# One attention layer on one core: the first stage in another order, weighted sums in one run, transposes three slots behind their scores

## The reference

```
# block 0: an adapter with one of 16 experts per sequence, then a layer norm
h   = gelu(x @ down_W.T + down_b)                 # 256 -> 64
h   = h @ expert_W[e].T + expert_b[e] + domain_emb[e]
x   = layernorm(h @ up_W.T + up_b + x) * gamma + beta
# block 1: attention with a bias, 16 heads of 16, then a feed-forward net
emb = silu(sin_cos(timestep)) @ W_ada + b_ada     # one row per sequence
x   = layernorm(x) * (1 + scale) + shift          # scale, shift = halves of emb
s   = q @ k.T / 4 + attention_bias                # 512 x 512 per head
p   = softmax(where(mask, -inf, s))
x   = x + (p @ v) @ Wo + bo
h   = layernorm(x) * g2 + beta2
out = x + gelu2(h @ W1 + b1) @ W2 + b2            # 256 -> 1024 -> 256
```

## Time and profile before

| | |
|---|---|
| median of three runs | 978.33 us (977.5 to 978.37) |
| profiled execution, its own time | 975.33 us |
| its span, first to last instruction | 973.4 us |
| PE busy | 904.8 us (93%) |
| DVE, ACT, POOL busy | 720.6, 702.2, 704.1 us (74, 72, 72%) |
| granted PE clock, mean | 0.972 of full speed |
| moved by DMA | 207.39 MB |

### The profile page before, as it was taken

How to read it: one execution, slowest core, us unless ns; L and a number is a source line. 1 busy time by engine, 2 the same in 40 slices (tenths; PEclk the granted TensorE clock), 3 DMA queues, 4 the chain that set the end, 5 groups by cost and what they waited for, 6 DMA issues and landing times.

```text
span 973.4 us, 20669 instructions
## 1 busy us (share of the span) xinstructions
PE 904.8 (93%) x6472; PEld 652.3 (67%) x6472; DVE 720.6 (74%) x1905; ACT 702.2 (72%) x1661; POOL 704.1 (72%) x407
## 2 busy tenths in 40 slices
PE   4648979999999999999999999999999999999986
PEld 1435545777677776777777776777777777677765
DVE  5738787878778787878778787878778787675642
ACT  2237758978788787878788787878788787877641
POOL 2448966888779886888769877878688886885700
PEclk8777989999999999999999999999999999999998
DMA  5499858876897669876797768876897668865300
GB/s 170 130 286 319 268 151 237 252 227 200 243 287 214 209 207 247 254 223 206 223 290 216 225 205 253 246 218 207 236 278 204 204 203 248 247 200 154 115 12 11
DMA packets 147948, 207.39 MB, mean 213 GB/s; under 512 B 14385, under 2 KB 62322, under 8 KB 147842
## 3 DMA queue, kind: packets, MB, share of 16 engines
q1 hardware_dynamic: 147842, 206.09, 71.7%
HBM read 185.05 MB, written 20.99 MB: 212 GB/s over the span
## 4 chain that ended last, share of the span: by engine, by line
PE 77%; DVE 2%; issue 2%; POOL 1%; ACT 1%; DVEq 0%; POOLq 0%; ACTq 0%
PE tp L834 19%; PE pv L791 12%; PE la L754 11%; PE sc L827 11%; PE lc L739 10%; PE lb L591 4%; PE lb L771 3%; PE lb L607 2%; DVE xm L1091 1%; PE lc L573 1%; POOL bias_s L494 1%; PE la L581 1%; PE la L565 1%; PE lb L565 1%; PE pv L802 1%
## 5 line engine op out<-in xcount | busy, mean ns | idle before, releaser
L494 POOL TENSOR_TENSOR bias_s<-mask_f,bias_s 128x1024 f32<-128x1024 f32 x256 | 602.3, 2371 | 159.6 <-DMA bias_s<-in_bias 159.0
L1360 DVE CUSTOM_DVE_ANT_0 bias_s<-sc,bias_s 128x512 f32<-128x512 f32 x512 | 349.1, 684 | 178.7 <-PE sc L827 166.1
L974 ACT ACTIVATE bias_s<-bias_s,mx 128x512 f32<-128x512 f32 x512 | 371.4, 726 | 115.9 <-DVE mx L1360 113.9
L834 PE MATMUL tp<-ident,bias_s 128*128 128x128 f32 x2048 | 311.6, 275 | 6.1 <-ACT pT L980 3.1
L834 PEld LDWEIGHTS tp<-ident,bias_s 128*128 128x128 f32 x2048 | 253.0, 142 | 87.3 <-issue 17.0
L980 ACT COPY pT<-tp 128x512 f32<-128x512 f32 x336 | 195.7, 583 | 91.2 <-PE tp L834 90.9
L827 PE MATMUL sc<-stk,stq 128*128 128x512 bf16 x512 | 197.3, 386 | 24.9 <-DVE mx L1360 20.4
L791 PE MATMUL pv<-pT,v_all 128*32 128x256 f32 x2048 | 138.4, 388 | 0.2 <-issue 0.2
L754 PE MATMUL la<-w_s,act_s 128*128 128x256 f32 x512 | 128.2, 380 | 0.2 <-DVE act_s L1317 0.2
L1367 DVE COPY pT<-tp 128x512 f32<-128x512 f32 x176 | 120.5, 684 | 4.3 <-PE tp L834 4.2
L739 PE MATMUL lc<-hT,w_s 128*128 128x256 f32 x464 | 120.8, 384 | 2.3 <-ACT hT L929 1.9
(11 more groups left out here) (172 smaller groups left out, 809.9 us busy)
## 6 DMA issues: line engine op xcount, KB each, us to landing
bias_s<-in_bias SPq DMA_DIRECT2D x256, 512.0 KB, 4.4
stq<-q_parts SPq DMA_DIRECT2D x128, 96.0 KB, 3.8
stk<-k_parts SPq DMA_DIRECT2D x128, 96.0 KB, 4.1
k_parts<-kb SPq DMA_DIRECT2D x32, 192.0 KB, 2.3
q_parts<-qb SPq DMA_DIRECT2D x32, 192.0 KB, 2.5
xT<-in_x_t SPq DMA_DIRECT2D x8, 512.0 KB, 6.2
k_parts<-kb SPq DMA_DIRECT2D x32, 128.0 KB, 2.3
stq<-q_parts SPq DMA_DIRECT2D x64, 64.0 KB, 4.0
```

Of the source, the lines that this page charges most:

```text
L494: pool.tensor_tensor(tile, mask_f[:, :, :], tile, ALU.subtract).then_inc(s["masked"], 1)
L834: last = pe.transpose(tp[n % 2][:, kt * P:(kt + 1) * P], bias_s[:, n // 2 % NB, n % 2, kt * P:(kt + 1) * P], ident[:, :])
L974: act.activation(tile, tile, ACT.Exp, bias=mx[:, t:t + 1], scale=-1.0, accum_out=sums[:, j, head_of(hh):head_of(hh) + 1]).then_inc(s["prob ...
L1360: dve.tensor_tensor_reduce(out=tile, in0=sc[t % 2][:, :], in1=tile, scale=1.0, scalar=BIG, op0=ALU.add, op1=ALU.min, accum_out=mx[:, t:t + ...
```

## The change

The change has five parts.

1. **Weighted sums in one run.** `weigh(g)` issues all 32 matmul records of a group at once, at 13.6, 21.6, 29.6 and 5.6. What follows it (spread, divide) stands a slot or less earlier.
2. **LAG = 3.** Each tile is transposed three slots behind its score. DVE_MOVES is shifted by one so that DVE moves stand in the same slots. In the last iteration DVE also moves tile 30.
3. **W1 preparation.** `shift_parts` and the eight `b1_diag` products leave iteration 1 and stand at the end of DVE's first stage.
4. **First stage in another order.** The seven other experts are prepared and folded before the norms end and not after the queries. Their copies go to ACT. The embedding product stands behind them. Weights for keys, queries and values are loaded from ACT's queue. SP loads the keys of a chunk as soon as its own stores have landed; ACT stores the first queries and loads them back. ACT computes one exponential of known values behind the second gelu, which brings the exponential's table in.
5. **Middle steps.** The row statistics `st2` no longer wait for ACT's copy `a_x2`, and the copy is issued behind `mv2`.

```
-LAG = 4
+LAG = 3
-DVE_MOVES = (8, 10, 11, 13, 15, 17, 20, 23, 24, 25, 27)
+DVE_MOVES = (9, 11, 12, 14, 16, 18, 21, 24, 25, 26, 28)
+LAST_DVE_MOVES = DVE_MOVES + (30,)
...
-             pv=((14.0, 15.0), (22.0, 23.0), (30.0, 31.0), (6.0, 7.0)), spread=(23.3, 7.3))
+             pv=(13.6, 21.6, 29.6, 5.6), spread=(22.3, 6.3))
...
-MID = dict(wo=(21.0, 21.6), x2=22.6, copy=23.0, st2=23.6, mv2=24.3, hn=27.0, ht=28.6)
+MID = dict(wo=(21.0, 21.6), x2=22.6, st2=23.6, mv2=24.3, copy=25.0, hn=27.0, ht=28.6)
...
-W1_AT = dict(parts=4.6, diag=(5.6, 12.0, 13.3, 14.6), sums=(18.0, 19.0), scale=(20.3, 21.3), lift=(22.0, 23.0))
+W1_AT = dict(sums=(18.0, 19.0), scale=(20.3, 21.3), lift=(22.0, 23.0))
...
+            def load_half_keys(b, g, e):
                 wait(sp, s["sc_ready"], TI * (2 * b - 1) + TG * (g + 1))
-                sp.wait_ge(s["k_out"], 64 * (2 * b + 2))
+                sp.wait_ge(k_out[g % 2], 32 * (2 * b + e + 1))
...
             store_keys(0)
-            store_queries(0)
+            load_half_keys(0, 0, 0)
             store_keys(1)
-            load_queries(0, 0)
-            load_keys(0, 0)
+            load_half_keys(0, 0, 1)
...
-                    for kt in range(2 * half, 2 * half + 2):
+                    for kt in range(KT):
...
             adapter_gelu(1)
+            act.activation(sm[:, 13, :], sm[:, 12, :], ACT.Exp, scale=-1.0)
             copy_rows(0)
+            copy_rows(1)
             keys(0, 0)
...
+            dve.wait_ge(s["experts_in"], 16 * (B - 1))
+            effective(1, B, "eff")
             center(0)
             center(1)
+            modulation()
             normalize(0)
...
             values(0)
+            shift_parts()
+            for ft in range(FT):
+                ins = dve.tensor_scalar(b1_diag[:, ft, :], ident[:, :], vec[:, VEC["b1"] + ft:VEC["b1"] + ft + 1],
+                                        None, ALU.mult)
+            ins.then_inc(s["w1_parts"], 1)
```

More of the change, by code:

```diff
@@ L77, in mid_at @@
     if m == NCH - 2:
[L78 removed]
+        at = dict(wo=(10.0, 10.3), x2=11.6, st2=12.3, mv2=13.3, copy=14.0, hn=16.0, ht=17.3)
     if m == NCH - 1:
[L80 removed]
+        at = dict(wo=(9.6, 10.0), x2=10.3, st2=10.6, mv2=11.0, copy=11.3, hn=12.0, ht=12.3)
     return absolute(at, m + 1)
@@ L121, in on_act @@
 def on_act(n):
-    return n % TI not in DVE_MOVES
+    return n % TI not in (LAST_DVE_MOVES if n // TI == NCH - 1 else DVE_MOVES)
 def moved(n, by_act):
-    return sum(on_act(k) == by_act for k in range(n % TI)) + n // TI * (21 if by_act else 11)
+    return sum(on_act(k) == by_act for k in range(n))
 def head_of(hh):
@@ L312, in build @@
         stk_in = [sem(f"stk_in{g}") for g in range(NG)]
+        k_out = [sem(f"k_out{m}") for m in range(2)]
         block = ctx.enter_context(nc.Block())
@@ L634, in _ @@
             turn_experts(0, 1, "turned0")
-            embedding()
             pe.wait_ge(s["up_in"], 32)
@@ L641, in _ @@
             adapter_up(1)
+            pe.wait_ge(s["eff"], 1)
+            turn_experts(1, B, "turned")
+            embedding()
+            pe.wait_ge(s["spread"], 1)
+            fold_expert(1, tp[1], 1)
+            for b in range(2, 4):
+                fold_expert(b, sc[1], b % 2)
+            for b in range(4, 6):
+                fold_expert(b, lb, b % 2)
+            for b in range(6, 8):
+                last = fold_expert(b, lc, b % 2)
+            last.then_inc(s["fold_sum"], 1)
+            pe.wait_ge(s["folded"], 2)
+            adapter_down(1, 0)
+            adapter_down(1, 1)
             turn_rows(0)
+            turn_rows(1)
             pe.wait_ge(s["k_w_in"], 16)
@@ L646, in _ @@
             keys(0, 1)
-            turn_rows(1)
+            pe.wait_ge(s["a_xt1"], 2)
+            keys(1, 0)
+            keys(1, 1)
             pe.wait_ge(s["scaled"], 1)
@@ L659, in _ @@
             values(0, 1)
-            adapter_down(1, 0)
-            adapter_down(1, 1)
-            pe.wait_ge(s["spread"], 1)
-            fold_expert(1, la, 0)
-            for b in range(2, 4):
-                fold_expert(b, sc[0], b % 2)
-            for b in range(4, 6):
-                fold_expert(b, pv, b % 2)
-            pe.wait_ge(s["d_q"], 1)
-            for b in range(6, 8):
-                last = fold_expert(b, tp[0], b % 2)
-            last.then_inc(s["fold_sum"], 1)
-            pe.wait_ge(s["folded"], 2)
-            pe.wait_ge(s["d_k"], 2)
+            pe.wait_ge(s["d_k"], 2)
+            pe.wait_ge(s["d_q"], 1)
             pe.wait_ge(s["d_v"], 1)
@@ L793, in weigh @@
                                              stop=(g % 2 == 1 and kt == KT - 1), tile_position=(0, 32 * h))
-                    if half == 1:
-                        last.then_inc(s["pv_done"], 1)
+                    last.then_inc(s["pv_done"], 1)
                 def spread_inverses(r):
@@ L814, in steps @@
                     for g in range(NG):
-                        if (prev if g == NG - 1 else attn) and t in AT["pv"][g]:
-                            weigh(g, AT["pv"][g].index(t))
+                        if (prev if g == NG - 1 else attn) and t == AT["pv"][g]:
+                            weigh(g)
                     for r in range(2):
@@ L889, in keys, with load @@
                     act.copy(kb[c % 2][:, 1, :], k_bank(c)[:, :]).then_inc(s["a_k1"], 1)
+            def load(sem_name, pairs):
+                for dst, src in pairs:
+                    act.dma_start(dst, src).then_inc(s[sem_name], 16)
+            act.wait_ge(s["vec_in"], 64)
+            load("norm_in", [(gamma_r[:, :], gamma.to_broadcast([P, D])), (beta_r[:, :], beta.to_broadcast([P, D]))])
+            load("k_w_in", [(wk_s[:, :, :], wk.rearrange("(c p) n -> p c n", p=P))])
+            load("q_w_in", [(wq_s[:, :, :], wq.rearrange("(c p) n -> p c n", p=P))])
+            load("v_w_in", [(wv_s[:, :, :], wv.rearrange("(c p) n -> p c n", p=P)),
+                            (bo_r[:, :], bo.to_broadcast([P, D])), (bv_r[:, :], bv.to_broadcast([P, D]))])
+            adapter_gelu(0)
             act.wait_ge(s["idx_ready"], 2)
@@ L899, in _ @@
             act.activation(wqf, wqf, ACT.Identity, scale=-0.25).then_inc(s["scaled"], 1)
+            act.wait_ge(s["fold_sum"], 2)
+            act.copy(fold[:, 1, :], tp[1][0:A + 1, D:2 * D])
+            act.copy(fold[:, 2:4, :].rearrange("p b d -> p (b d)"), sc[1][0:A + 1, :])
+            act.copy(fold[:, 4:6, :].rearrange("p b d -> p (b d)"), lb[0:A + 1, :])
+            act.copy(fold[:, 6:8, :].rearrange("p b d -> p (b d)"), lc[0:A + 1, :]).then_inc(s["folded"], 1)
+            adapter_gelu(1)
+            act.activation(sm[:, 13, :], sm[:, 12, :], ACT.Exp, scale=-1.0)
             copy_rows(0)
+            copy_rows(1)
             keys(0, 0)
-            copy_rows(1)
             keys(0, 1)
+            keys(1, 0)
             queries(0, 0)
+            keys(1, 1)
             queries(0, 1)
-            keys(1, 0)
-            keys(1, 1)
-            adapter_gelu(1)
+            act.wait_ge(s["d_q"], 1)
+            for m in range(2):
+                act.dma_start(q_d[0, m].rearrange("n p t -> p n t"), qb[:, :, m * CH:(m + 1) * CH]
+                              ).then_inc(s["q_out"], 16)
+            act.wait_ge(s["q_out"], 32)
+            for row, parts, _ in RUNS:
+                act.dma_start(stq[row:row + parts * HD, 0:GH, :], q_rows[0, 0, 0:parts * HD, 0:GH, :]
+                              ).then_inc(stq_in[0], 16)
             def body(i, attn, prev, nxt, pre, qv, down):
```

114 lines of the change are left out of this document (42 added, 72 removed).

## The result

The changed kernel takes 961.66 us (median of four runs, 960.01 to 964.4) where the kernel before takes 977.91 us on the same chip: a ratio of 0.9837, 95% interval 0.9811 to 0.9864. It is faster by 16.2 us; 24.3 us were forecast. The profiled execution took 960.01 us, its span is 958.2 us. PE is now busy 890.0 us where it was 904.8 us.

A forecast was written before the change was run, and what follows sets the result against it. PE's own instructions bound late iterations, transfers iteration 0, and a chain over all engines the first stage. Terms 13.4 + 0.5 + 8.5 + 0 + 0 + 1.9 = 24.3 us took the median from 978.33 to 954.0 us, range 946.5 to 961.5.

The forecast's parts named there:

- W1's preparation: Iteration 1: moving DVE's W1 work to the first stage, away from POOL, saves 8.5 us, bounds 6.5 and 12.
- Weighted sums in one run: Iterations 2 to 15: one entry and exit fewer saves 0.24 us a group, 13.4 us; iterations 0 and 1 add 0.5.
- LAG = 3 at nothing: Loop: transposing a slot sooner costs nothing, covered by slack of 0.7 us in the worst tile; bounds 2.2 us lost, or 0.
- The end: Kernel's end: st2 no longer waits 0.65 us and one slot less is owed, 1.2 us; together 1.9 us saved.
- Iteration 0 at nothing: Iteration 0: transfers bind it and their bytes and order stay, so 0 us; bounds -4 to +2.
- The first stage at nothing, bounds of 3 us: Up to the first score: late modulation and gains sum to about +0.6 us, taken as 0, 3 us either way.
- a first score after 55 us: Sign at the end of the first stage that would show the prediction wrong; it expected the first score at 52 +- 2 us.
- the first adapter output comes about 3.7 us sooner: First stage: expert 0 no longer waits behind the embedding product (3.45 us), so the output, at 17.24 us before, comes sooner.
- leave SP's row, some 2 us: From last key store to first score: three loads of keys and three of queries, 0.45 us each, leave SP's row.
- The term of the keys at the high clock: First stage: PE is in work ahead of the keys and should run them about 1.9 us faster.
- 24.3 / 56: Rival of bursts behind the longer run: from 0.45 us of PE waits a group on, the kernel gets slower; 3%.
- worse, the late modulation is not recovered, 957.5 us: Rival for the first stage or iteration 0: the late modulation is not made up, giving 957.5 us; 12%.

The follow-up runs named there:

- only_w1: Kernel before with only shift_parts and the eight b1_diag products moved to the end of DVE's first stage; 967.35 us, ratio 0.9907.
- loads_late: Changed kernel with ACT's seven weight loads issued only when expert 0's load has landed; 960.65 us, ratio 0.9849.
- store_order: Changed kernel plus the three repairs of that chain, with chunk 1's two needed key stores ahead of chunk 0's key loads, its others behind all six; 958.07 us.
- rows_order: Like store_order, and PE transposes rows of chunks 0 and 1 ahead of the adapter of chunks 2 and 3; 955.52 us, ratio 0.9789.
- old_order: The change with the first stage of before, but chunk 1's two other key stores behind the six key loads in SP's row; 953.61 us, ratio 0.9756.
- three repairs of that chain: Changed kernel with embedding product ahead of seven transposes, ACT's loads behind expert 0's, expert 0's copy ahead of turns_of_angles; together 958.75 us, ratio 0.9823.
- after_bias: Changed kernel with the loads of bias tiles 2 to 5 ahead of the exchange of keys in SP's row; 958.03 us, ratio 0.9825.

## Why the prediction was right or wrong

**Direction and mechanisms of the loop: right.** W1's preparation was to give 8.5 us and gave 8.58 in the trace of the change, 9.1 us alone. The eight products took 1.66 us (1.8 forecast), 0.21 us each, with POOL idle. As the Trainium skill has it (SBUF — State Buffer, SBUF: two separate sides), DVE and GpSimd hold a common port pair in turn; the pairs of 4.30 us in the earlier trace rows and 0.46 us beside no mask agree. No wait of PE in iteration 1 is above 1.31 us, and it takes 52.55 us (52 forecast).

**Weighted sums in one run: right in mechanism, a tenth too large.** 0.24 us a group was forecast. Late iterations fell by 0.88 us, 0.22 a group (53.48 to 52.60, 55.78 to 54.90 us), which makes 12.3 us for 56 groups in place of 13.4. Two of them fell less: iteration 14 by 0.32 us and iteration 6 by 0.60. The rows around one run still add up to 1.96 us a group, 0.24 less than before; the 0.02 between the two is within their rounding.

**LAG = 3 at nothing: right, with its cover.** Without the runs it loses 0.28 us in each odd iteration, as the lack of 0.17 us said, and in the change nothing, as the 0.86 us of the longer run said. "No growth of L830's waits for ACT" holds.

**The end: too large.** With iteration 15's four groups (1.0 us) it was to give 2.9 us, and it gave 1.3 us in one pair of executions; the end of before, 97.50 us from the start of iteration 15, took 98.25 us in only_w1, which has the same code there. st2 waits no longer. But the last products came sooner than the wide inverses, and PE waits 0.98 us for ACT's copy (`rwide`), a wait that the forecast had not seen.

**Iteration 0 at nothing: right for the change** (0.3 us), but the sentence "its bytes and order on SP stay the same from the first score on" stopped one step short. What counts is how much has landed ahead of the first score.

**The first stage at nothing, bounds of 3 us: wrong, and this is the step that failed.** It was +6.2 us in the traces and some 6 us by the ratios (0.9777 against 0.9837), and this term alone puts the time out of the forecast's own 3 us. The time lies only 0.16 us over the range's end at 961.5. The prediction had named the sign: a first score after 55 us, and it came at 58.58. Three steps of the term failed. First, "the first adapter output comes about 3.7 us sooner": it came 0.38 us sooner, because seven loads from ACT's queue (4.19 to 7.6 us) stood beside expert 0's, which took 5.5 us from issue to use in place of 2.1 (loads_late), because the copy stood behind turns_of_angles, and because the adapter ran at the low clock, 2.07 us where it took 1.13. Second, modulate(0) was to be 3.3 to 5.3 us late and was 8.76 us late: the embedding ended at 30.5 and not at 25.6 us, 3.3 us from the first failure and 1.7 us from the slower adapter. Third, "leave SP's row, some 2 us": nothing came of it. The way from the store to the first score took 8.78 us in place of 8.25, and store_order, rows_order and old_order show no gain from SP's order there. SP's last key store is issued by 52.80 us and the loads of those keys only at 54.07: what is waited for is the landing of stores, and then of loads. The term of the keys at the high clock, -1.9 us, was right at -1.8.

**The sum.** 24.3 us were forecast. The first stage took 6.2 of them; the runs and the end together gave 12.8 us in place of 15.8 (1.3 us too much in iterations 2 to 14, 0.2 in 0 and 1, 1.5 from iteration 15 on), and W1 gave 0.1 us more than forecast; that leaves the 15.2 us of the spans. One slip in the rivals changes nothing: 24.3 / 56 is 0.43 us and not 0.45. The rival "worse, the late modulation is not recovered, 957.5 us" (12%) named the cause; it was too small by 4 us. That three repairs of that chain gave back little (1.4 us by the ratios, 0 to 5 by their intervals) led to a second one of like length, which none of the cases had: rows behind the adapter of chunks 2 and 3, worth 2.6 us. What the late score costs, the forecast had not asked of iteration 0: there the transfers that had not run ahead of it had to be made up.

**Open.** Why executions of one and the same first stage differ by 3 us at the first score; how exactly the 6 us divide between idle transfers and a late score, since the estimate of 4.6 us comes from two executions and both move together in most of these kernels; and whether after_bias would keep its gain if POOL were not behind in iteration 1.

## What to carry to other kernels

In a preamble that ends in a stage bound by transfers, ask of each change when the DMA engines next stand idle, and put the big loads with no dependence ahead of the small ones that wait: four loads moved up in SP's row gave some 6 us by the ratios with the old first stage, more than any single reordering of compute here, though only 2.8 and 1.2 us with the new one. Check what the next stage gives back. A chain to which a product is appended must be costed from the trace's landing times, and a cut in it is worth only the distance to the next chain, less what a lower clock takes back. Build the parts of a mixed change apart: here the loop's parts gave 22 us, and the first stage took 6 back.
